# Two attention layers and their gated MLPs: from four stages in a row to one unrolled stage of 64 tiles

## The reference, cut to what matters

```python
def _layer(x, wqkv, qs, ksc, wo, lg, lb, w1, b1, w2, b2):
    h = shift_token(x)            # upper 64 of 128 features come from the token before
    q, k, v = jnp.split(h @ wqkv, 3, axis=-1)          # then to 8 heads
    q = l2norm(q) * qs; k = l2norm(k) * ksc
    q, k = rotary_xpos(q, k)
    o = local_attention(q, k, v)
    x = x + o @ wo
    h = shift_token(x)
    h = (h - mu) / jnp.sqrt(var + 1e-05) * lg + lb
    a, g = jnp.split(h @ w1 + b1, 2, axis=-1)
    return x + (a * jax.nn.gelu(g, approximate=False)) @ w2 + b2
# the block: y = _layernorm(x); y = _layer(y, layer 0); y = _layer(y, layer 1); x + y
```

## Time and profile before

| | before |
|---|---|
| median of 3 runs | 1866.24 us (1866.13 to 1867.06) |
| the profiled execution: its time, its span | 1866.51 us, 1864.7 us |
| mean granted TensorE clock | 0.921 of full speed |
| busy share of the span | PE 78%, DVE 71%, ACT 57%, POOL 49% |
| `normalise` begins loading | 1015.98 us |
| first instruction of `attend_first`, of `attend_second` on DVE | 1036.48, 1449.70 us |
| last addition of `gated_mlp_second` | 1861.02 us |

### The profile page before, as it was taken

How to read it: one execution, slowest core, us unless ns; L and a number is a source line. 1 busy time by engine, 2 the same in 40 slices (tenths; PEclk the granted TensorE clock), 3 DMA queues, 4 the chain that set the end, 5 groups by cost and what they waited for, 6 DMA issues and landing times. The chain is left out here.

```text
span 1864.7 us, 26805 instructions
## 1 busy us (share of the span) xinstructions
PE 1445.9 (78%) x8740; PEld 800.6 (43%) x8740; DVE 1316.6 (71%) x1932; ACT 1061.9 (57%) x1849; POOL 917.2 (49%) x468
## 2 busy tenths in 40 slices
PE   6755299667577777777679689999789689999789
PEld 2314288323122223222233256666634366666533
DVE  2954133266799999999721699999633699999534
ACT  4431155487656666566444677887542587887442
POOL 0431433103888988888500277767400466776300
PEclk8875599887799999999989899999979899999989
DMA  1007111300000000000001000000010000000001
GB/s 58 0 6 158 58 46 34 91 0 1 0 1 1 0 1 0 0 0 0 0 12 48 3 1 2 0 0 0 1 61 0 1 2 2 0 0 0 13 6 40
DMA packets 35020, 30.08 MB, mean 16 GB/s; under 512 B 7763, under 2 KB 29573, under 8 KB 34566
## 3 DMA queue, kind: packets, MB, share of 16 engines
q1 hardware_dynamic: 32646, 24.48, 5.0%
q0 software_dynamic: 2304, 4.74, 0.8%
HBM read 19.73 MB, written 9.47 MB: 16 GB/s over the span
## 5 line engine op out<-in xcount | busy, mean ns | idle before, releaser
L1550 POOL TENSOR_TENSOR at_direct<-at_direct,at_square 128x1024 f32<-128x1024 f32 x64 | 152.5, 2383 | 412.4 <-DVE at_square L1608 412.4
L1023 POOL TENSOR_TENSOR ssm_dbu<-ssm_dtu,ssm_b_all 128x1024 f32<-128x1024 f32 x128 | 298.5, 2360 | 21.6 <-ACT ssm_b_all L976 21.1
L884 PE MATMUL ssm_bank<-ssm_seen,ident 128*128 128x512 f32 x512 | 247.4, 606 | 45.1 <-POOL ssm_seen L1031 37.7
L971 ACT ACTIVATE ssm_bank<-ssm_dt,ssm_decay 128x512 f32<-128x512 f32 x256 | 176.8, 691 | 118.0 <-DVE ssm_state L1122 115.6
L1389 PE MATMUL at_ps<-at_wqkv,at_hs 128*128 128x512 f32 x384 | 187.9, 628 | 32.8 <-ACT at_hs L1486 17.6
L1122 DVE TENSOR_TENSOR_SCAN ssm_state<-ssm_bank,ssm_dbu 128x512 f32<-128x512 f32 x128 | 147.9, 1204 | 15.4 <-POOL ssm_dbu L1023 15.1
L1122 DVE TENSOR_TENSOR_SCAN ssm_state<-ssm_bank,ssm_carry,ssm_dbu 128x512 f32<-128x512 f32 x128 | 155.3, 1263 | 1.9 <-POOL ssm_dbu L1023 1.6
L884 PEld LDWEIGHTS ssm_bank<-ssm_seen,ident 128*128 128x128 f32 x512 | 95.8, 193 | 131.0 <-issue 63.9
L1555 POOL TENSOR_TENSOR at_prob<-at_prob,at_inv 128x1024 f32<-128x1024 f32 x64 | 121.4, 1897 | 21.8 <-DVE at_inv L1618 21.8
L1564 POOL TENSOR_TENSOR at_direct<-at_direct,at_rnorm 128x1024 f32<-128x1024 f32 x64 | 131.4, 2053 | 0.5
L1389 PEld LDWEIGHTS at_ps<-at_wqkv,at_hs 128*128 128x128 f32 x384 | 71.4, 199 | 108.0 <-issue 75.9
(11 more groups left out here) (240 smaller groups left out, 3418.0 us busy)
## 6 DMA issues: line engine op xcount, KB each, us to landing
moe_w<-in_moe_w SPq DMA_DIRECT2D x16, 256.0 KB
moe_to_experts<-moe_empty SPq DMA_DIRECT2D x10, 258.0 KB, 8.0
moe_slot_rows<-moe_to_experts SPq DMA_DIRECT2D x10, 258.0 KB, 3.0
x<-in_x SPq DMA_DIRECT2D x8, 256.0 KB, 3.4
moe_rows<-moe_from_experts SPq DMA_DIRECT2D x8, 256.0 KB, 4.5
at_turn<-in_turn SPq DMA_DIRECT2D x2, 1024.0 KB
out_x<-x SPq DMA_DIRECT2D x8, 256.0 KB, 2.0
at_wqkv<-in_wqkv SPq DMA_DIRECT2D x2, 768.0 KB
```

The costliest lines, as they stand in the source:

```text
L884: last = nc.tensor.matmul(bank[Y0 + half][:], ident[:], seen[:, n % 2, half], start=n == 0, stop=False)
L971: nc.scalar.activation(bank[DA0 + half][:], dt[:, half, cols(b * 2 + k)], ACT.Exp, scale=decay[:, half, n:n + 1]).then_inc(s[f"da{half}"], 1)
L1023: nc.gpsimd.tensor_tensor(dbu[:, n % RING], dtu[:, k], b_all[:, n % 2:n % 2 + 1, :].broadcast_to([P, 2, CH]), ALU.mult).then_inc(s["dbu"], 1)
L1550: nc.gpsimd.tensor_tensor(direct[:, quarter], direct[:, quarter], crossed[:, half], ALU.add).then_inc(s["added"], 1)
```

## The change

The four stages behind `normalise` become one stage, `ffn`, written out fully: steps g = 0 to 76 over 64 tiles, 32 of layer 0 and then 32 of layer 1, with the lags of before. A chunk of 4 tiles enters its MLP behind its attention. `FIRST` is 9, and `chunk_at(g, k)` gives the chunk c with g = 9 + 4c + k, so each step holds the pieces of one phase of four:

- phase 0: `values` 0 and 1 of the chunk before, the output product `to_rows` in two halves (now on 512 columns at once, 4 products in place of 16), DVE's `prods` 0 and 1 and the addition `attended`.
- phase 1: `values` 2, `down` 0 and 1, `prods` 2, all of the chunk before; `centring` and ACT's square of this one.
- phase 2: `down` 2 and `leave` of the chunk before; `variance`, Ln, Exp (`root`) and `normed` of this one.
- phase 3: three `gates` products, and on ACT `gelus`: a table load, three Gelus, a table load back.

PSUM is dealt out anew: `two` (2 banks) serves the transposes of q and k, then the q and k projection, then the transposes of the probabilities, three times in every step; `one` serves the v projection and the value product; `scores` has 2 banks, the MLP 3. ACT's copies into `hs` and ACT's and DVE's copies into `v_mix`, and DVE's shift for the second LayerNorm (`hs2`), become DMAs from SBUF to SBUF, issued by SP. Each table switch stands in the middle of the attention work. The output is stored chunk by chunk. All weights of both layers are loaded in `normalise`: 36 issues on SP where 11 were. The final `x + branch` moves to POOL.

```diff
-STAGES = [min_gru, experts, mamba, mlp, normalise, attend_first, gated_mlp_first, attend_second, gated_mlp_second]
+STAGES = [min_gru, experts, mamba, mlp, normalise, ffn]
-    layer_norm(nc, mem, "norm", mem["x"], mem["branch"], loads=attend_loads(mem, dram, 0))
+    layer_norm(nc, mem, "norm", mem["x"], mem["branch"],
+               loads=attend_loads(mem, dram, 0) + attend_loads(mem, dram, 1))
 # PE, a step of ffn
+            for g in range(LAST + 1):
+                n = g - SCORE
+                if real(n):
+                    pe.wait_ge(s["scaled"], up_to(n))
...
+                if chunk_at(g, 4) is not None:
+                    values(chunk_at(g, 4), (0, 1))
+                if chunk_at(g, 0) is not None:
+                    to_rows(chunk_at(g, 0), (0, 1))
+                if chunk_at(g, 5) is not None:
+                    values(chunk_at(g, 5), (2,))
+                if chunk_at(g, 6) is not None:
+                    down(chunk_at(g, 6), (2,))
+                if chunk_at(g, 2) is not None:
+                    variance(chunk_at(g, 2))
+                if chunk_at(g, 3) is not None:
+                    gates(chunk_at(g, 3))
...
+                    if real(n):
+                        pe.wait_ge(s["kT_copied"], up_to(n))
...
+                n = g - VALUE
+                if real(n):
+                    pe.wait_ge(s["weighted"], up_to(n))
+                    if real(g):
+                        pe.wait_ge(s["qk_copied"], up_to(g))
...
+                if chunk_at(g, 5) is not None:
+                    down(chunk_at(g, 5), (0, 1))
+                if chunk_at(g, 0) is not None:
+                    to_rows(chunk_at(g, 0), (2, 3))
+                if chunk_at(g, 1) is not None:
+                    centring(chunk_at(g, 1))
...
+                if real(n):
+                    pe.wait_ge(s["pT_copied"], up_to(n))
 # ACT
+            def gelus(c):
+                act.preload_act_table_set("gelu_and_others")
+                if c >= 1:
+                    act.wait_ge(s["down"], up_to(c - 1))
+                for p, (first, size) in enumerate(HID_PARTS):
+                    act.wait_ge(s["gates"], c * PARTS_OF_HID + p + 1)
+                    nc.scalar.activation(hidden[0:size, p], glu[PART_BANK[p]][0:size, :], ACT.Gelu,
+                                         bias=b1[0:size, c // LAYER_CHUNKS, 1, p:p + 1]).then_inc(s["gelu"], 1)
+                act.preload_act_table_set("natural_log_exp_and_others")
 # SP, a step of ffn
+                    sp.wait_ge(s["attended"], up_to(c))
...
+                    sp.dma_start(hs2[0:64, q % 2, k * CH:(k + 1) * CH], of[0:64]).then_inc(s["hs2"], 16)
+                    sp.dma_start(hs2[64:128, q % 2, 1 + k * CH:1 + (k + 1) * CH], of[64:128]).then_inc(s["hs2"], 16)
...
+                    sp.dma_start(v_mix[0:64, g % HELD], v[0:64, g % HELD]).then_inc(mixed[g % 2], 16)
+                    sp.dma_start(v_mix[64:128, g % HELD], v[64:128, (g - 1) % HELD]).then_inc(mixed[g % 2], 16)
```

More of the change, by code:

```diff
@@ L1306, in attend_loads @@
+    if layer == 0:
+        loads += [(mem["eye16"][:], dram["eye16"]), (mem["mask"][:], dram["mask"])]
+    for c, (first, size) in enumerate(HID_PARTS):
+        loads.append((mem["w2"][0:size, layer, c], dram["w2"][layer, first:first + size]))
     for n, name in enumerate(("q_scale", "k_scale")):
         row = dram[name][layer:layer + 1]
-        loads.append((mem["scales"][:, 0, n], row.partition_broadcast(P)))
+        loads.append((mem["scales"][:, layer, 0, n], row.partition_broadcast(P)))
@@ L1329, in attend, with up_to, ffn @@
+def up_to(n, each=1):
+    return (n + 1) * each
+def ffn(nc, mem, dram):
+    x, branch, ident, centre, mean = (mem[name] for name in ("x", "branch", "ident", "centre", "mean"))
     with ExitStack() as ctx:
         def sb(name, shape, dt=F32):
[L1331 to L1335, removed]
+            return ctx.enter_context(nc.sbuf_tensor(f"at_{name}", shape, dt))
+        wqkv, wo, eye16, mask, turn, scales, w1, w2, ln_g, ln_b, b1, b2 = (mem[name] for name in (
+            "wqkv", "wo", "eye16", "mask", "turn", "scales", "w1", "w2", "ln_g", "ln_b", "b1", "b2"))
+        hs = sb("hs", [P, 2, 1 + T])
+        hs2 = sb("hs2", [P, 2, 1 + T])
@@ L1363, in _ @@
         @block.tensor
         def _(pe):
[L1365 to L1409, removed]
@@ new lines, in _ @@
+            for layer in range(LAYERS):
+                for m in range(2):
+                    for p, (first, size) in enumerate(HID_PARTS):
+                        at = (layer * 2 + m) * PARTS_OF_HID + p
+                        last = nc.tensor.matmul(glu[0][0:size, at:at + 1],
+                                                w1[:, layer, m * HID + first:m * HID + first + size],
+                                                ln_b[:, layer:layer + 1], start=True, stop=True)
+            last.then_inc(s["lb_done"], 1)
@@ new lines, in up, with gates @@
+            def up(c, m, p, to):
+                first, size = HID_PARTS[p]
+                return nc.tensor.matmul(glu[to][0:size, :],
+                                        w1[:, c // LAYER_CHUNKS, m * HID + first:m * HID + first + size],
+                                        normed[:], start=True, stop=True)
+            def gates(c):
+                pe.wait_ge(s["normed"], up_to(c))
+                pe.wait_ge(s["logged"], up_to(c))
+                if c >= 1:
+                    pe.wait_ge(s["branch"], up_to(c - 1))
+                for p in range(PARTS_OF_HID):
+                    up(c, 1, p, PART_BANK[p]).then_inc(s["gates"], 1)
@@ L1434, in step @@
                     last.then_inc(s["sim"], 1)
[L1435 to L1445, removed]
@@ L1458, in step @@
                     for pair in range(4):
[L1459 removed]
+                        for q, values_of in ((0, v_mix), (1, v)):
                             for odd in range(2):
```

711 lines of the change are left out of this document (409 added, 302 removed).

## The result

The changed kernel takes 1893.43 us (median of 4 runs, 1891.35 to 1895.05), the one before 1866.18 us beside it (4 runs, 1865.59 to 1867.06). The ratio is 1.0145, with a 95% interval of 1.0127 to 1.0163: 27 us slower, outside the range. The profiled execution took 1891.35 us, 1.75 more than its span, at a granted clock of 0.899.

A forecast was written before the change was run, and what follows sets the result against it. PE was taken as the bound: 1121.2 to its step 9, then 42.8, 562.8, 32.7, 40.1 and 30.6 make 1830.2; 22 for the clock gives a span of 1852.6, predicted as 1854 us, range 1824 to 1882.

The forecast's parts named there:

- PE becomes the bound: In the new stage, PE has 40.8 us of work per chunk without waits, against 36 on DVE.
- The ring through `two`: Per step, PE and ACT take turns on `two`: 8.4 us without a piece, 46.9 a chunk, 3.3 idle in phase 3.
- The clock in phase 3: Behind PE's 3.3 us idle spell in every chunk the clock falls; bounds 0 to 3.2 us, 1.6 taken.
- The shorter case: Earlier trace, PE after 2.33 us idle: six instructions took 4.37 us where 2.74 is normal, giving 1.6 per chunk.
- The rival on the other side: Two half-clock stretches per chunk, the second over phase 0, costing 3.2 us or more each chunk: 1877 us; chance 0.21.
- the hand sum: PE's four phases counted in the new stage: 46.9 us per chunk, 11.7 per tile, without clock loss.
- The first rival: In phase 3 the clock does not fall, or falls where PE waits anyway: 1832 us; chance 0.24.
- The load: Before `ffn`, SP's 36 issues at 0.46 us take 16.6; the stage begins at 1043.2, a loss of 6.7.
- The dearer switch: ACT's table switches in phase 3 each have a load-length gap behind: 14 x 2.6 us more, 1890; chance 0.04.
- The starved engine: The long straight code starves an engine: 0.3 us lost a step would give 1875 us; chance 0.03.
- PE without waits: ACT's work overlaps better than counted, so PE takes 40.8 us a chunk: about 1753 us; chance 0.04.
- The transfers cost nothing: SP's SBUF-to-SBUF DMAs for `v_mix` and `hs2` arrive before they are wanted and add no time.

The follow-up runs named there:

- the filled version: The change plus four unused 512-column products on PE per phase 3, three behind the scores and one in the wait for `pT`: 1851.78 us.
- the late loads: The change with 13 of layer 1's 17 loads issued inside the stage and its tables built at step 20: 1879.76 us.
- the order by shape: In opening tiles, all 64-row value products before the 128-row ones, added to the change with switch and Gelus moved behind `pT`: 1817.45 us.

## Why the prediction was wrong

The sum, against the trace: PE's step 9 was forecast at 1121.2 and came at 1128.03 (6.8 late); steps 9 to 63 were to take 659.1 with the clock and took 691.1 (32.0 more); the end from step 64 was to take 72.3 and took 70.5 (1.8 less). That is the whole difference of 37.0 between spans.

- **PE becomes the bound: right.** Busy 89% in the middle where DVE has 67%. DVE was taken at 75%; the longer period makes more than half of the difference.
- **The ring through `two`: right in its mechanism.** PE's wait in phase 3 was forecast at 3.3 and is 3.38, the wait for `pT` 1.2 and is 1.11. Phases 2, 1 and 3 are 10.08, 10.6 and 15.2 or 16.05 in turn (14.35 with a whole clock) against 10.1, 10.4 and 14.2. The sum of a chunk was 1.0 us short: half of it is the slow value product of an opening tile (1.0 every second chunk), which the sum had at the price of any other tile; 0.2 each are in phases 0 and 1, 0.15 in phase 3.
- **The clock in phase 3: the step that failed.** "The shorter case gives six instructions 1.6 us; I take 1.6 per chunk, since part of the stretch lies on waits". Filling the spell gave back 3.3 a chunk. Little of the stretch lies on waits: PE is busy 5.87 of 6.80 us in one chunk and 7.98 of 10.24 in the next. The right row was there, in the earlier trace rows: 6.5 us of low clock behind 3.11 idle, with PE busy 5.5. The short case from the earlier trace rows was chosen although the spell in question (3.38, then 1.11 more) is longer than either of its examples. With 3.3, a little above the upper bound of 3.2, the sum is 1852.6 + 14 x 1.7 = 1876. The 14 is one too many: step 64 has no projection and no such spell, and the first chunk's low stretch lasted 3.4 us only.
- **The rival on the other side came true in place and price**: low clock over the dense phase 0, at more than the 2.5 us a chunk from which it decides. It is one stretch of 6.8 or 10.2 us, though, not the two that this rival named. Its 1877 lacked the 6.8 us of the fill and the 1.0 a chunk of the hand sum (14 us), which brings it to 1898, near the 1893 measured. The first rival, a clock that does not fall, is out by the 0.92. A recurring wait that lowers the clock in every turn of a loop is what the Trainium skill describes in "TensorE: Matmul & The Clock Gate", section "HAM oscillation — how this bites in real kernels", for waits on transfers. Here the wait is for another engine's copy, and the trace agrees: every one of the 3.4 us spells in the middle stretch has half clock behind it.
- **The load: right in kind, too small.** 0.46 us an issue gave 16.6 for 36; they took 23.9 (1015.87 to 1039.80), because some took up to 3.76. The stage began at 1047.1 instead of 1043.2. The other 2.9 us until step 9 are the fill; 2.4 of them went with the late loads and tables.
- **The dearer switch**: out, by the rows of the loads. **The starved engine**: no sign of it; with a whole clock the straight code keeps to the hand count within 1.0 in 47.9 us. **PE without waits**: out, by 56 us of waits in 500.
- **The transfers cost nothing**: right for `v_mix`, by the run without them; for `hs` and `hs2` no run leaves them out.

Where the expected gain went: with the clock whole, the forecast's sum was a span of 1830.2, 34.5 us under the kernel before. The hand sum's shortfall takes 14 of that and load and fill 6.8, which leaves 14; the filled version, with its clock whole in the stage, is 14.2 under it in spans (1850.5 against 1864.7). The clock then takes 39 us (1889.6 against 1850.5) and turns the gain into a loss. This account holds to some 2 us: the stages that all three share ended 2.3 us later in the profiled execution of the filled version than in that of the change.

## What to carry to other kernels

When engines share one bank in turn, cost each step by what stands ahead of the bank's next reader on its own in-order engine. A table switch with its functions belongs where nothing on that ring is behind it: here that moved the kernel from 1893 to 1825 us, and the load back, moved out of the way as well, gave another 19. (The rest of the way to 1787 is the order by shape, 8, and the late loads, 11.) Price an idle spell of TensorE that comes back in a loop as the spell plus the work at half clock behind it, by the row in the trace whose spell is as long, above all where the work behind is dense. If the wait can't be moved, unused products in it may pay for themselves: four of them gave 42 us, one gave 11.

## What was not expected of the hardware

Products with 64 and with 128 rows of weights in turn start their groups of four 0.26 us apart, against 0.12 in one shape; eight groups take 2.1 us in place of 1.1. Sorting them by shape gave 7.6 us for eight tiles. The 19 DMA issues of layer 0 on SP took 9.6 us, 0.50 each; the 17 of layer 1 right behind them took 14.4, 0.84 each, and the load of `turn` 3.76 where its twin in layer 0 took 0.50. Issued inside the stage instead, 13 of the 17 took 6.4 us, 0.49 each. What the slow ones waited for is not shown. And four products that nobody reads, 3.4 us of work in each chunk, made the kernel 42 us faster.
